# A state-space, attention and tree-router tower on one core: the last table doubling in two halves, and chunk 11 beside the first qkv step

## The chip, the core and the metric

The kernel runs on one core of a Trainium2 chip. Five engines work side by side: TensorE (PE) multiplies matrices, VectorE (DVE) and ScalarE (ACT) work on rows of 128 partitions, GpSimd (POOL) does elementwise work too, and SyncE (SP) mainly issues transfers. Each engine takes its instructions strictly in the order in which they were written for it, and waits for the others through semaphores. The metric is the device time of one execution in microseconds.

## The reference, cut to what matters

H = 256 channels, N = 64 states, 256 lags, 16 signals per channel. The output is a sum of three stages; the change touches the first and the place where it meets the second.

```
dA = (1 + dtA/2) / (1 - dtA/2)                 # one complex number z per channel and state
V  = exp(log(dA) * arange(256))                # its powers z^0 .. z^255
K  = 2 * real(einsum('chn,hnl->chl', C * B, V))     # the tokens: h
h  = h + attention_block(layernorm(h))         # norm, qkv, linear attention, proj, MLP
h  = h + tree_router(layernorm(h))
```

## The kernel before

**Tables.** A lag l is split into three digits, l = 64 d + 8 a + e with d < 4 and a, e < 8, so that z^l is a product of three table entries. `U` holds z^64, z^128 and z^192, `Er` and `Ei` hold z^1 to z^7, and `X` and `Y` (together `XY`, 8 values of each for every channel) hold B times z^(8a). The powers z, z^2, z^4 ... come from a chain of squarings between VectorE (L1088, L1090) and ScalarE (L662, L665). `X` and `Y` start with one value per channel and are doubled three times on VectorE (L1099 to L1120): 1 to 2, 2 to 4, 4 to 8 values, each time multiplied with a power that ScalarE has copied into PSUM. The last doubling is five instructions over all 256 channels. GpSimd makes z^3 (six instructions in `rotated`), then z^5 to z^7 for the first 128 channels (`shifted(0)`), then rotates chunks 0 and 1, then makes z^5 to z^7 for the other channels (`shifted(1)`).

**Fixed products.** Before the first chunk TensorE makes three products of weights alone: the gate's (L1715), the leaf values' (L1721) and a bias of the MLP (L1727, 16 groups of one column). It starts them when the weights' loads have landed and VectorE has passed a count (`DVE_POWERS + 8`). The first chunk's matmuls wait until ScalarE has copied the bias out of bank 0 (`b1copied`).

**Chunks.** The channels go in 16 chunks of 16. For each chunk n: SyncE loads the coefficients (`craw`, a direct and two crossed parts); GpSimd multiplies them with `U` into `Wa` and `Wb` (`rotate`, L514); ScalarE copies the chunk's `XY` to PSUM (`tables`), and the unrotated parts of `Wa` and `M` (`operands`); VectorE makes two products (L1130) and adds them into `M` (L1148, L1170); TensorE does 64 small matmuls (`tokens`, L1628); ScalarE copies the result to `tokev` (`token_row`, or `closed` with the store to a scratch in device memory). Chunk 10 is an exception: VectorE leaves its two products unadded (`unsummed_products`) and TensorE adds them with 128 matmuls instead of 64 (`unsummed_tokens`, L1646 and L1648).

**Steps.** The scratch is read back with the channels on the partitions (`load_h0`, tiles s = 0 to 15, of which 0 to 7 need chunks 0 to 7 only). A step s of the attention stage is: `norm1_stats(s)` on VectorE, `scales(s)` on GpSimd (three instructions, the last a power), `norm1_apply(s)` into `xh`, `y_transposes(s)` on TensorE, `y_high(s)` on ScalarE, `y_low(s)` on VectorE, then `q_products(s)` and `kv_products(s, 0 and 1)` on TensorE, with what ScalarE (`q_parts`, `kv_parts`) and VectorE (`q_elu`, `k_elu`) make of them. The chunks 12 to 15 run between steps 0 to 3. After them come the other steps, and then the loop of the MLP and the router.

**Order.** It is written by hand for each engine; nothing is moved by a scheduler. `CREDIT` is only a constant that is added to the loop semaphores. The names in what follows: W(n) is `rotate` of chunk n, M(n) the sum on VectorE, tokens(n) the matmuls.

## Time and profile before

| | us |
|---|---|
| time, median of 3 runs | 491.57 (491.56 to 491.72) |
| the profiled execution's own time | 492.88 |
| its span, first to last instruction | 491.1 |
| TensorE busy | 442.3 (90%) |
| VectorE busy | 346.6 (71%) |
| ScalarE busy | 294.8 (60%) |
| GpSimd busy | 191.5 (39%) |
| mean granted clock of TensorE | 0.968 of full |

The times below are microseconds from the start of the span. A row of the timeline gives start, duration, engine, line, operation, tiles and count, and in square brackets how long the engine had been idle before and what ended that. Operations on one engine overlap a little, so the step from one start to the next is a better price than the duration. Tile numbers are left out, so all banks of PSUM read as PS.

### The profile page before, as it was taken

How to read it: one execution, taken by the hardware profiler on the slowest of the kernel's cores; microseconds unless marked ns; L12 is line 12 of the kernel's file. 1: busy time of each engine (PE TensorE's matmuls, PEld its weight loads, DVE VectorE, ACT ScalarE, POOL GpSimd, SP SyncE). 2: the span in 40 equal slices, each digit the busy share in tenths (PEclk: the TensorE clock that was granted, in tenths of full speed). 3: DMA queues.
4: the chain of work that ended last, by engine and by line, in shares of the span. 5: the costliest groups of instructions: out<-in, count | busy, mean ns of one | idle time of the engine just before them, and what ended most of it. 6: DMA issues, size and time to landing. Idle time of an engine off the chain costs nothing.

```text
span 491.1 us, 11436 instructions
## 1 busy us (share of the span) xinstructions
PE 442.3 (90%) x3881; PEld 404.0 (82%) x3881; DVE 346.6 (71%) x814; ACT 294.8 (60%) x617; POOL 191.5 (39%) x188
## 2 busy tenths in 40 slices
PE   0475778999999999999999999999999999998995
PEld 0165667887888898988998998998998998998994
DVE  4899996996877785546586486486486576574675
ACT  4734654889876776466366366366367367356551
POOL 0299997742432110515405405406406306306120
PEclk9965999999999999999999999999999999999995
DMA  4532668445352111001002002002002001001002
GB/s 129 185 137 71 177 175 223 109 111 157 101 119 89 63 44 35 31 1 44 1 2 85 0 0 85 0 0 85 0 0 85 0 0 43 0 0 45 1 1 85
DMA packets 39903, 30.95 MB, mean 63 GB/s; under 512 B 19520, under 2 KB 35264, under 8 KB 39872
## 3 DMA queue, kind: packets, MB, share of 16 engines
q1 hardware_dynamic: 28944, 27.48, 18.9%
q10 hardware_dynamic: 10928, 3.08, 2.7%
q8 instruction: 16, 0.26, 0.2%
q14 instruction: 15, 0.12, 0.1%
...
## 4 chain that ended last, share of the span: by engine, by line
PE 69%; DVE 12%; issue 6%; POOL 4%; ACT 4%; DMA 3%; SPq 1%; DVEq 0%; POOLq 0%; ACTq 0%
PE PS L336 19%; PE PS L338 18%; PE PS L337 18%; PE PS L1655 5%; PE PS L1697 3%; PE PS L1628 2%; POOL Wb L514 2%; DVE XY L1055 2%; DVE bst L1357 2%; DMA craw<-in_c_ri 1%; DMA aim<-in_a_im 1%; PE PS L1664 1%; PE PS L1780 1%; DVE gl L1380 1%; DVE PS L1055 1%
## 5 line engine op out<-in xcount | busy, mean ns | idle before, releaser
L867 ACT ACTIVATE PS<-PS,fc1bias 128x512 f32<-128x512 f32 x56 | 36.7, 655 | 76.3 <-PE PS L338 76.2
L336 PE MATMUL PS<-fc2h,gh 128*128 128x256 f32 x256 | 74.7, 292 | 3.7 <-DVE gl L1380 2.3
L567 POOL TENSOR_SCALAR pst<-mv 128x4 f32<-128x4 f32 x15 | 4.2, 282 | 179.4 <-DVE pst L1364 179.4
L338 PE MATMUL PS<-fc2l,gh 128*128 128x256 f32 x256 | 71.4, 279 | 0.0
L337 PE MATMUL PS<-fc2h,gl 128*128 128x256 f32 x256 | 71.3, 278 | 0.0
L1380 DVE TENSOR_TENSOR gl<-PS,gh 128x512 fp32r<-128x512 f32 x56 | 38.6, 690 | 37.8 <-ACT gh L870 35.1
L336 PEld LDWEIGHTS PS<-fc2h,gh 128*128 128x128 f32 x256 | 48.0, 188 | 9.0 <-DVE gl L1380 3.0
L336 PE MATMUL PS<-x2Th,fc1h 128*128 (+2 forms) x144 | 54.5, 378 | 0.0
L337 PE MATMUL PS<-x2Th,fc1l 128*128 (+2 forms) x144 | 53.0, 368 | 0.0
L338 PE MATMUL PS<-x2Tl,fc1h 128*128 (+2 forms) x144 | 52.9, 367 | 0.0
L337 PEld LDWEIGHTS PS<-fc2h,gl 128*128 128x128 f32 x256 | 48.2, 188 | 0.8
L338 PEld LDWEIGHTS PS<-fc2l,gh 128*128 128x128 f32 x256 | 48.1, 188 | 0.0
L1628 PE MATMUL PS<-M,Wa 128*64 128x64 f32 x480 | 32.0, 233 | 11.7 <-ACT Wa L717 4.3
L1628 PEld LDWEIGHTS PS<-M,Wa 128*64 128x64 f32 x480 | 29.8, 143 | 14.4 <-issue 9.6
L870 ACT ACTIVATE gh<-PS 128x512 fp32r<-128x512 f32 x56 | 33.5, 599 | 2.8
L1628 PE MATMUL PS<-M,Wb 128*64 128x64 f32 x480 | 31.5, 230 | 0.0
L338 PEld LDWEIGHTS PS<-x2Tl,fc1h 128*128 128x128 f32 x144 | 27.1, 189 | 4.7
L1628 PEld LDWEIGHTS PS<-M,Wb 128*64 128x64 f32 x480 | 29.8, 146 | 0.0
L336 PEld LDWEIGHTS PS<-x2Th,fc1h 128*128 128x128 f32 x144 | 27.2, 189 | 2.5
L337 PEld LDWEIGHTS PS<-x2Th,fc1l 128*128 128x128 f32 x144 | 27.2, 189 | 2.3
L514 POOL TENSOR_TENSOR Wa<-craw,U 128x768 f32<-128x768 f32 x16 | 26.0, 1623 | 3.4 <-DMA craw<-in_c_ri 1.5
L336 PE MATMUL PS<-qkvh,yh 128*128 128x512 f32 x64 | 26.4, 412 | 0.0
(256 smaller groups left out, 1412.9 us busy)
## 6 DMA issues: line engine op xcount, KB each, us to landing
...
```

What stands on the lines that cost most here:

```text
L336: pe.matmul(dst, ah, bh, start=start, stop=False, **kw)
L337: pe.matmul(dst, al, bh, start=False, stop=False, **kw)
L338: return pe.matmul(dst, ah, bl, start=False, stop=stop, **kw)
L514: pool.tensor_tensor(w[:, par, :, :, 1:ND].rearrange("p h c d -> p d h c"), c, u, ALU.mult).then_inc(wdone, 1)
L867: act.activation(bank(j % 2), bank(j % 2), ACT.Gelu, bias=fc1bias[:, j:j + 1]).then_inc(gact, 1)
L870: act.activation(gh[:, j % 2, :], bank(j % 2), ACT.Copy).then_inc(gact, 1)
L1055: link(dve.tensor_tensor(out_, a, b, op))
L1357: dve.bn_stats(bst[:, t, :], x[:, t, :]).then_inc(done, 1)
L1380: dve.tensor_tensor(gl[:, j % 2, :], bank(j % 2), gh[:, j % 2, :].bitcast(F32), ALU.subtract).then_inc(gldone, 1)
L1628: mm = pe.matmul(dst, w[:, par, i, :, :].rearrange("p c d -> p (c d)"), M[:, par, i, :, :].rearrange("p a e -> p (a e)"), start=x == 0, st ...
L1655: mm = pe.transpose(PS[:, b + k, t * P:(t + 1) * P], src[:, t, k * P:(k + 1) * P], ident)
L1697: mm = pe.matmul(PS[:, sums_bank(c), k * (P + 1):(k + 1) * (P + 1)], key, value, start=half == 0 and k == 0, stop=half == 1, skip_group_ch ...
```

## The change

It has six parts.

1. **First loads.** `aim` was loaded by two DMAs on ScalarE's queue. Now its two halves go on the two queues, in front of the 768 KB of `qkvraw`, and two of the four `btab` loads move to ScalarE's queue.
2. **Powers.** z^3 is made in `pw` and already after `DVE_Z + 6`, beside the chain of squarings; `shifted` reads `pw` and `pw4` and no longer waits for ScalarE's copies. Those eight copies to `Er` and `Ei` come later. Five imaginary parts are written to PSUM by VectorE, and ScalarE copies fewer of them.
3. **Last doubling in halves.** Channels 0 to 127 are doubled before chunk 0, channels 128 to 255 between M(7) and the products of chunk 8. ScalarE's `tables` of chunks 8 and 9 wait for that (`DVE_XY`).
4. **Chunk 10 is summed on VectorE** as the others are, and `unsummed_tokens` is gone.
5. **Chunk 11** goes behind step 0's first `kv_products` on TensorE. W(11) stands behind `scales(0)`, and `norm1_stats`, `norm1_apply`, `y_high` and `tables` are in another order.
6. **Waits and loads.** The fixed products start at `DVE_POWERS + 10`, and the last quarter of the bias's products waits for the first product of chunk 0. SyncE loads tile 0 of h0 before the coefficients of chunks 10 and 11, and the coefficients of chunk 12 before tiles 2 and 3.

```diff
-DVE_W1 = DVE_U + 3
+DVE_XY = DVE_U + 5
+DVE_W1 = DVE_XY + 3
 DVE_W2 = DVE_W1 + 2 + KD
 POOL_TABLES = 1 + 2 * 6
+GATE = 10
...
+        def u_imag(d):
+            return (PS[:, 2, H:2 * H], PS[:, 3, 0:H], PS[:, 3, H:2 * H])[d]
+
         def power(j):
 
-            if j < 3:
+            if j < 2:
                 return [pw[:, j, x, :] for x in range(2)]
+            if j == 2:
+                return [pw4[:, x, :] for x in range(2)]
             if j < 6:
-                return [pwb[:, j - 3, x, :] for x in range(2)]
-            return [U[:, 0, j - 6, :], ui[:, j - 6, :]]
+                return [pwb[:, j - 3, 0, :], (PS[:, 6, H:2 * H], PS[:, 7, H:2 * H], PS[:, 2, 0:H])[j - 3]]
+            return [U[:, 0, j - 6, :], u_imag(j - 6)]
...
-            sp.dma_start(qkvraw[:, :, :], qkvT.rearrange("(k p) o -> p k o", p=P)).then_inc(ld_qkv, 16)
+            sp.dma_start(aim[halves[1], :], a_im).then_inc(ld_aim, 16)
             for r, rows in enumerate(halves):
                 sp.dma_start(btab[rows, 0, :], b_ri[r]).then_inc(ld_b, 16)
-                sp.dma_start(btab[rows, 1, :], b_ri[1 - r]).then_inc(ld_b, 16)
+            sp.dma_start(qkvraw[:, :, :], qkvT.rearrange("(k p) o -> p k o", p=P)).then_inc(ld_qkv, 16)
...
-            for n in range(2, FIRST):
+            for n in range(2, SINGLE):
                 load_c(n // 2, n % 2)
             for par in range(2):
                 sp.wait_ge(h0st[par], CREDIT + 16 * (PAIRS // 2))
-            for s in range(4):
+            load_h0(0)
+            for n in range(SINGLE, FIRST):
+                load_c(n // 2, n % 2)
+            load_h0(1)
+            load_c(FIRST // 2, FIRST % 2)
+            for s in range(2, 4):
                 load_h0(s)
-            load_c(FIRST // 2, FIRST % 2)
             store_h0(SINGLE)
...
-            pool.wait_ge(dve_set, DVE_POWERS)
-            rotated(Er[:, :, 2], Ei[:, :, 2], pw[:, 0, 0, :], pw[:, 0, 1, :], pw[:, 1, 0, :], pw[:, 1, 1, :],
+            pool.wait_ge(dve_set, DVE_Z + 6)
+            rotated(pw[:, 2, 0, :], pw[:, 2, 1, :], pw[:, 0, 0, :], pw[:, 0, 1, :], pw[:, 1, 0, :], pw[:, 1, 1, :],
                     tE[:, :, 0])
-            pool.wait_ge(e_out, 6)
-            wr, wi = (pw[:, 2, x, :].unsqueeze(2).to_broadcast([P, H, 3]) for x in range(2))
+            wr, wi = (pw4[:, x, :].unsqueeze(2).to_broadcast([P, H, 3]) for x in range(2))
 
             def shifted(half):
                 hs = slice(half * P, (half + 1) * P)
-                rotated(Er[:, hs, 4:7], Ei[:, hs, 4:7], Er[:, hs, 0:3], Ei[:, hs, 0:3], wr[:, hs, :], wi[:, hs, :],
-                        tE[:, hs, :])
+                ar, ai = (pw[:, :, x, hs].rearrange("p e h -> p h e") for x in range(2))
+                rotated(Er[:, hs, 4:7], Ei[:, hs, 4:7], ar, ai, wr[:, hs, :], wi[:, hs, :], tE[:, hs, :])
...
             rotate(SINGLE // 2, 0)
-            rotate(SINGLE // 2, 1)
             scales(0)
             pool.wait_ge(xh1, CREDIT + 2)
+            rotate(SINGLE // 2, 1)
             rotate(FIRST // 2, 0)
...
             act.dma_start(iar[N:P, :], inv_ar).then_inc(ld_exp, 16)
+            act.dma_start(aim[0:N, :], a_im).then_inc(ld_aim, 16)
             for r in range(2):
-                act.dma_start(aim[r * N:(r + 1) * N, :], a_im).then_inc(ld_aim, 16)
+                act.dma_start(btab[r * N:(r + 1) * N, 1, :], b_ri[1 - r]).then_inc(ld_b, 16)
...
+            act.activation(PS[:, 6, 0:H], pwb[:, 0, 0, :], ACT.Copy).then_inc(pw_out, 1)
+            act.wait_ge(dve_set, DVE_POWERS + 4)
             for d in range(ND - 1):
-                if d == 2:
-                    act.wait_ge(dve_set, DVE_POWERS + 4)
-                act.activation(U[:, 1, d, :], ui[:, d, :], ACT.Copy, scale=sgn[:, 0:1]).then_inc(u_out, 1)
-
+                act.activation(U[:, 1, d, :], u_imag(d), ACT.Copy, scale=sgn[:, 0:1]).then_inc(u_out, 1)
+            act.activation(pwb[:, 2, 1, :], PS[:, 2, 0:H], ACT.Copy).then_inc(u_out, 1)
+            act.activation(PS[:, 7, 0:H], pwb[:, 1, 0, :], ACT.Copy).then_inc(pw_out, 1)
...
+            act.wait_ge(pool_set, 1 + 6)
+            for e in range(4):
+                for x, t in enumerate((Er, Ei)):
+                    w = pw4[:, x, :] if e == 3 else pw[:, e, x, :]
+                    act.activation(t[:, :, e], w, ACT.Copy).then_inc(e_out, 1)
...
+            act.activation(PS[:, 6, H:2 * H].rearrange("p (x h) -> p x h", x=2), pwb[:, 2, :, P:H],
+                           ACT.Copy).then_inc(pw_out, 1)
+            act.wait_ge(pe_set, 2)
+            act.activation(leafraw[:, :, :].rearrange("p k x -> p (k x)"), bank(5), ACT.Copy).then_inc(staged, 1)
...
+            with act.Fori(0, 2) as it:
                 for par in range(2):
                     next_opened(it, par)
-            paired_tables(4, 1)
+            next_opened(2, 0)
+            paired_operands(3, 1)
+            closed(2, 1)
+            m_unshifted(3, 1)
             closed(3, 0)
             paired_operands(4, 0)
+            closed(3, 1)
+            act.wait_ge(dve_set, DVE_XY)
+            for par in range(2):
+                paired_tables(4, par)
             m_unshifted(4, 0)
-            closed(3, 1)
             paired_operands(4, 1)
             m_unshifted(4, 1)
             tables(SINGLE)
+            closed(SINGLE // 2 - 1, 0)
             operands(SINGLE)
-            closed(SINGLE // 2 - 1, 0)
-            tables(SINGLE + 1)
             closed(SINGLE // 2 - 1, 1)
             operands(SINGLE + 1)
+            tables(SINGLE + 1)
+            y_high(0)
+            tables(SINGLE + 2)
             token_row(SINGLE)
-            tables(SINGLE + 2)
             operands(SINGLE + 2)
-            y_high(0)
             for n in range(FIRST, CHUNKS):
                 s = n - FIRST
+                if s == 0:
+                    q_parts(s)
...
+            dve.wait_ge(pw_out, 1)
+            doubled(slice(0, H), 1, *halves_of(6), bank(0))
+            dve.wait_ge(pw_out, 2)
+            dve.wait_ge(u_out, 4)
+            doubled(slice(0, H), 2, *halves_of(7), PS[:, 2:4, :].rearrange("p b x -> p (b x)"))
+            dve.wait_ge(pw_out, 3)
+            doubled(slice(0, P), 4, *(w[:, 0:P] for w in halves_of(1)), bank(2))
...
-            for n in range(6, SINGLE - 1):
-                overlapped(n, n % 2)
-            product_sums(SINGLE - 1, 1)
+            overlapped(6, 0)
+            product_sums(7, 1)
+            dve.wait_ge(pw_out, 4)
+            doubled(slice(P, H), 4, PS[:, 6, H:H + P], PS[:, 6, H + P:2 * H], bank(2))
+            assert count[0] == DVE_XY, count[0]
+            dve.wait_ge(pool_set, POOL_TABLES + 6)
+            for n in (8, 9):
+                first_product(n, n % 2)
+                second_product(n, n % 2)
+                product_sums(n, n % 2)
...
-            unsummed_products(SINGLE)
+            norm1_stats(0)
+            single_product(SINGLE, 0)
+            single_product(SINGLE, 1)
+            single_sums(SINGLE)
+            norm1_apply(0)
             single_product(SINGLE + 1, 0)
             single_product(SINGLE + 1, 1)
-            norm1_stats(0)
+            y_low(0)
             single_sums(SINGLE + 1)
-            norm1_apply(0)
             norm1_stats(1)
-            norm1_stats(2)
-            y_low(0)
             for n in range(FIRST, CHUNKS):
                 s = n - FIRST
                 single_product(n, 0)
+                if s == 0:
+                    norm1_stats(2)
+                    norm1_apply(1)
                 single_product(n, 1)
+                single_sums(n)
                 if s == 0:
-                    norm1_apply(1)
                     norm1_apply(2)
...
-            pe.wait_ge(dve_set, DVE_POWERS + 8)
+            pe.wait_ge(dve_set, DVE_POWERS + GATE)
...
+                if j == JH * 3 // 4:
+                    pe.wait_ge(prodX, CREDIT + 1)
...
-            unsummed_tokens(SINGLE)
             y_transposes(0)
-            pe.wait_ge(tokout, CREDIT + SINGLE + 1)
-            tokens(SINGLE + 1, 1, None)
+            pe.wait_ge(tokout, CREDIT + SINGLE - 1)
+            tokens(SINGLE, 0, 0)
             pe.wait_ge(qkvld, 3)
             for n in range(FIRST, CHUNKS):
                 s = n - FIRST
                 if s > 0:
                     y_transposes(s + 1)
                 q_products(s)
+                if s == 0:
+                    pe.wait_ge(tokout, CREDIT + SINGLE)
                 kv_products(s, 0)
                 if s == 0:
+                    pe.wait_ge(tokout, CREDIT + SINGLE + 1)
+                    tokens(SINGLE + 1, 1, 0)
                     y_transposes(s + 1)
                 kv_products(s, 1)
                 pe.wait_ge(tokout, CREDIT + n)
-                tokens(n, n % 2, None)
+                tokens(n, n % 2, 0)
```

VectorE, from M(7) on, in the kernel before (XY is the table, PS the banks, Mb and Mc hold second products, bst and mv the statistics of a tile of h0):

```order
L1130 TENSOR_TENSOR Mb<-PS,Ei 128x896 [waits vdone]
L1130 TENSOR_TENSOR PS<-PS,Er 128x896 [waits vdone,xyld]
L1148 TENSOR_TENSOR M<-PS,Mb 128x128x7 [waits prodY,prodX,tokmm]
L1130 TENSOR_TENSOR Mc<-PS,Ei 128x896 [waits vdone]
L1148 TENSOR_TENSOR M<-PS,Mc 128x128x7 [waits prodY,prodX,tokmm]
L1130 TENSOR_TENSOR M<-PS,Er 128x128x7 [waits vdone,tokmm,xyld]
L1130 TENSOR_TENSOR Mc<-PS,Ei 128x896
```

And now, from M(7) to M(8):

```order
L1177 TENSOR_TENSOR M<-PS,Mc 128x128x7 [waits prodY,prodX,tokmm]
L1074 TENSOR_TENSOR XY<-XY,PS 128x256x4 [waits pw_out]
L1074 TENSOR_TENSOR PS<-XY,PS 128x512 [waits dve_set]
L1074 TENSOR_TENSOR XY<-XY,PS 128x128x4 [waits dve_set]
L1074 TENSOR_TENSOR PS<-XY,PS 128x512 [waits dve_set]
L1074 TENSOR_TENSOR XY<-XY,PS 128x128x4 [waits dve_set]
L1159 TENSOR_TENSOR PS<-PS,Er 128x896 [waits xyld,vdone,pool_set,dve_set]
L1159 TENSOR_TENSOR Mb<-PS,Ei 128x896 [waits vdone]
L1177 TENSOR_TENSOR M<-PS,Mb 128x128x7 [waits prodY,prodX,tokmm]
```

Five instructions of the doubling stand between M(7) and chunk 8, and chunk 8's products are no longer made ahead of the sum before them.

GpSimd from W(11) on, in the kernel before (Wa and Wb make one W; pst and mr are `scales`):

```order
L514 TENSOR_TENSOR Wa<-craw,U 128x3x256 [waits tokmm,cld1]
L514 TENSOR_TENSOR Wb<-craw,U 128x3x256 [waits crossld1]
L522 ISA
L522 TENSOR_SCALAR pst_94<-mv_93 128x2 [waits st1]
L523 TENSOR_SCALAR pst_94<-mv_93 128x2
L525 TENSOR_TENSOR mr<-pst_94,halfpow 128x2x2 [waits r1done]
L514 TENSOR_TENSOR Wa<-craw,U 128x3x256 [waits cld0,xh1,tokmm]
```

And now, from behind W(10) on:

```order
L529 ISA
L529 TENSOR_SCALAR pst_94<-mv_93 128x2 [waits st1]
L530 TENSOR_SCALAR pst_94<-mv_93 128x2
L532 TENSOR_TENSOR mr<-pst_94,halfpow 128x2x2 [waits r1done]
L521 TENSOR_TENSOR Wa<-craw,U 128x3x256 [waits cld1,xh1,tokmm]
L521 TENSOR_TENSOR Wb<-craw,U 128x3x256 [waits crossld1]
L521 TENSOR_TENSOR Wa<-craw,U 128x3x256 [waits tokmm,cld0]
L521 TENSOR_TENSOR Wb<-craw,U 128x3x256 [waits crossld0]
L529 TENSOR_SCALAR pst_94<-mv_93 128x2 [waits st1]
```

`scales(0)` has moved in front of W(11), which now stands together with W(12) behind the wait for step 0's `xh`.

## Rows read from the trace of the kernel before

**Rows 1.** Busy time of each engine in a stretch, then TensorE's granted clock.

```profile
97.00:103.80 6.80, 6.80 (x94) 5.98 (x92) 6.63 (x15) 5.96 (x15) 4.61 (x6) 1.00 0.45 122
```

**Rows 2.** Chain that ended last: start, us, what.

```profile
1.97 6.12 DMA aim<-in_a_im
...
88.12 2.10 PE PS L1628 x64
90.23 0.59 PE PS L1664 x4
```

**Rows 3.** Timeline of VectorE, from the tables to step 0.

```profile
6.04 0.43 DVE L1068 SCALAR_TENSOR_TENSOR base<-base 128x256 f32<-128x256 f32 x1 [3.41 <-ACT base L644]
8.18 0.42 DVE L1070 SCALAR_TENSOR_TENSOR base<-aim,base 128x256 f32<-128x256 f32 x1 [1.72 <-DMA aim<-in_a_im]
...
27.53 0.69 DVE L1055 TENSOR_TENSOR XY<-XY,PS 128x512 f32<-128x512 f32 x1
...
28.97 3.54 DVE L1055 TENSOR_TENSOR XY<-XY,PS 128x1024 f32<-128x1024 f32 x2
32.55 1.23 DVE L1055 TENSOR_TENSOR PS<-XY,PS 128x1024 f32<-128x1024 f32 x1
...
38.17 1.10 DVE L1130 TENSOR_TENSOR PS<-PS,Er 128x896 f32<-128x896 f32 x1 [0.62 <-ACT PS L722]
39.18 1.08 DVE L1130 TENSOR_TENSOR Mb<-PS,Ei 128x896 f32<-128x896 f32 x1
...
78.26 0.74 DVE L1213 TENSOR_SCALAR xh<-h,mv,mr 128x256 f32<-128x256 f32 x2 [0.83 <-issue]
...
84.52 0.74 DVE L1213 TENSOR_SCALAR xh<-h,mv,mr 128x256 f32<-128x256 f32 x2
...
86.89 1.08 DVE L1170 TENSOR_TENSOR M<-PS,Mb 128x896 f32<-128x896 f32 x1
```

**Rows 4.** Timeline of TensorE: gate product, tokens(0), tokens(8).

```profile
27.03 3.78 PE L1715 MATMUL PS<-routraw,wqraw 128*128 128x256 f32 x8 [9.35 <-DMA fc1raw<-in_fc1T]
...
41.63 0.49 PE L1628 MATMUL PS<-M,Wa 128*64 128x64 f32 x4 [3.93 <-DVE M L1148]
...
66.95 0.34 PE L1628 MATMUL PS<-M,Wa 128*64 128x64 f32 x4 [0.89 <-POOL Wb L514]
```

**Rows 5.** TensorE in stretches: length, busy, granted clock, DMA.

```profile
17.70:22.00 4.30, 0.00 (x0) 1.00 0.82 232
23.00:27.00 4.00, 0.00 (x0) 0.50 1.01 377
27.00:33.00 6.00, 5.97 (x14) 0.50 0.38 131
...
42.00:45.00 3.00, 3.00 (x62) 0.50 0.16 52
64.00:66.00 2.00, 2.00 (x64) 1.00 0.69 183
```

**Rows 6.** Timeline of GpSimd: W(2), W(10), `scales(0)`, W(12), `scales(1)`, W(13).

```profile
45.72 1.61 POOL L514 TENSOR_TENSOR Wa<-craw,U 128x768 f32<-128x768 f32 x1 [0.64 <-PE PS L1628]
...
69.53 1.63 POOL L514 TENSOR_TENSOR Wa<-craw,U 128x768 f32<-128x768 f32 x1
...
76.54 0.24 POOL L522 TENSOR_SCALAR pst<-mv 128x2 f32<-128x2 f32 x1 [0.96 <-DVE mv L1205]
...
79.64 1.64 POOL L514 TENSOR_TENSOR Wa<-craw,U 128x768 f32<-128x768 f32 x1 [1.48 <-DMA craw<-in_c_ri]
...
82.82 0.22 POOL L522 TENSOR_SCALAR pst<-mv 128x2 f32<-128x2 f32 x1
...
87.18 1.62 POOL L514 TENSOR_TENSOR Wa<-craw,U 128x768 f32<-128x768 f32 x1 [1.04 <-DVE xh L1213]
```

**Rows 7.** Timeline of ScalarE: token row of chunk 7, what follows its store.

```profile
66.16 0.60 ACT L736 ACTIVATE tokev<-PS 128x512 f32<-128x512 f32 x1 [0.88 <-PE PS L1628]
...
67.30 0.71 ACT L717 ACTIVATE Wa<-craw 128x256 f32<-128x256 f32 x1 [0.55 <-ACT tokev L736]
```

87 lines of the change are left out of this document (27 added, 60 removed).

## The prediction

> **What bounds the kernel now.** I first read the busy time by stretches. From 97.0 to 103.8 us TensorE is busy 6.80 of 6.80 us at full clock [rows 1], and the chain that ended last has TensorE in it from tokens(12) at 88.12 and `y_transposes(2)` at 90.23 on [rows 2]. From there the order of work is the same in both kernels. So the change is worth what `y_transposes(2)` comes earlier, and the question is what holds the time before it. The timelines answer that. Up to 38 us it is VectorE's tables, behind `aim`, which lands 6.12 us after its issue [rows 2, 3]. Then GpSimd sets the pace: W(2) starts at 45.72, when tokens(0) is done, and W(10) at 69.53, eight chunks in 23.81 us, 2.98 each, without a wait [rows 6]. VectorE has three operations for each chunk, 1.0 us apart [rows 3], so it has no slack to speak of. After W(11) it is a load, `scales` and `xh`: W(12) waits for its coefficients until 79.64, `scales(1)` starts at 82.82, `xh(1)` at 84.52, M(12) at 86.89 [rows 3, 6].
>
> **The first loads.** VectorE is ready for `aim` at 6.04 + 0.43 = 6.5 and starts at 8.18 [rows 3]. The gain is between 0 and 1.67 us. The half that landed late was issued third on its queue, while 768 KB ran on the other. Both halves are now ahead of that block, and their nearest neighbour is `iar`, issued just ahead, which had landed and been used by 6.04 [rows 3]. I take 1.67.
>
> **The half doubling.** The last doubling is now 2.31 us (3.54 less the 1.23 of the step before) and four of 1.23, together 7.2. Half of it is one of 1.23 and four of 0.69 [rows 3], with gaps 4.1. So the first product comes 3.2 us earlier, at 38.17 - 1.67 - 3.2 = 33.3, and VectorE would let tokens(0) start at 41.63 - 4.85 = 36.8 [rows 3, 4]. z^3 and the first shift on GpSimd hide behind this, since they start nine VectorE steps of 0.43 sooner and the 1.67 besides: 5.5 us. ScalarE's late copies of `Er` and `Ei` hide in the time in which it has nothing else before the first `tables`. I cost both at nothing; without the cover each would hold up the first product.
>
> **The fixed products take over as the bound of tokens(0).** Before they started at 27.03, when `fc1raw` had landed, and ended 3.93 us ahead of tokens(0), at 37.7 [rows 4]. Now they wait for the load and for the second instruction of the second doubling: 27.53 + 0.69 - 1.67 = 26.55. They start at 26.7 at the earliest and end at 37.4; with the copy of the bias tokens(0) would start at 37.8. But from 27 to 33 us the clock was at 1.2 GHz [rows 5]. That is six us of their 10.7, so a rise two us sooner saves one. The bounds are 36.8 (VectorE) and 37.8. I take 37.0, near the lower, because the rise in this trace came only 6 us after their start, and leaves more room for an earlier one than for a later.
>
> **tokens(0) to W(10).** At half clock tokens(0) starts 4.09 us before W(2) [rows 4, 6]; at full clock 64 matmuls take 2.1 [rows 2], so this would be 2.7. In the trace tokens(0) ran at 0.50 [rows 5], 3.93 us behind the bias products, which stream one column each; the pause is gone now, the thin products ahead of it are not. I take half again: W(2) at 41.1, 4.6 earlier. GpSimd is free by then: its own work ended at 45.72 - 0.64 = 45.1, and by the 5.5 us above now ends at 39.6. The same 4.6 us hold up to chunk 7: its token row moves from 66.16 to 61.55 [rows 7]. Here the second half costs. ScalarE's next operation comes 1.14 us after the start of the token row, behind the store [rows 7]: `tables(8)` at 62.7. VectorE has done M(7) at 57.5 (24 operations since 33.3, and 0.2) and the doubling at 61.6, so the 4.1 us are hidden behind TensorE and ScalarE. But chunk 8's products, which were made ahead before, start only now: 0.6 us behind `tables` (0.62 at 38.17), and from the first product to the matmuls it is 3.3 more (41.63 - 38.17, less a short wait) [rows 3, 4]. tokens(8) starts at 66.6 against 66.95. Of 4.6 us there are 0.35 left.
>
> **The new gap on TensorE.** Between tokens(7), done at 61.4, and tokens(8) TensorE now stands still for 5.2 us; before it was 0.89 [rows 4]. In the stretches the clock was full from 17.7 to 22 us, in a pause that began at 17.7, and at half from 23 on: after some 5.3 us [rows 5]. The pauses of 0.9 us between chunks left it full, as from 64 to 66. So I take the clock to fall in the gap, and tokens(8) to run at half: W(10) comes 4.1 us behind its start, at 70.7, against 69.53. At full clock it would be at 69.3. The Trainium skill, "TensorE: Matmul & The Clock Gate", section on HAM oscillation, says that bursts of matmuls with waits between them let the clock fall back, so that each burst begins slow. That speaks against this change at this place. By the page's rule the sum is the one taken here; if the clock took no note of the gap, as it took none of the pauses of 0.89 us, it would be 1.4 us less.
>
> **W(10) to the steady steps.** The chain of prices: from W to the `scales` behind it 3.18 (79.64 to 82.82); `scales` to `xh` 1.72 (76.54 to 78.26); `xh` to the next W 0.94 [rows 3, 6]; a W 2.98. So `scales(0)` is at 73.9, `xh(0)` 75.6, W(11) 76.55, W(12) 79.5, `scales(1)` 82.7, `xh(1)` 84.4. The load for W(12) is now issued before two tiles of h0 and no longer waited for. Behind `xh(1)` stand 0.7 us of its own and the second product, 1 us, which has moved there: M(12) at 86.2 against 86.89. Then `xh(2)`, 0.6 us, has moved between M(12) and `y_low(1)`, so `y_transposes(2)` waits for that and starts at 89.6 against 90.23 [rows 2]. Chunk 10's sum on VectorE is another 1 us, and spares TensorE the 64 extra matmuls; both lie under the wait for `xh(0)`, which GpSimd's `scales(0)` sets. Chunk 11's 2 us between the two `kv_products` fit in, because TensorE would wait for `xh(1)` there.
>
> **Sum.** 90.23 - 89.6 is 0.6 us, of a profiled execution of 492.88. The timed runs have a median of 491.57, 1.3 lower; I apply the difference to the median: **490.9 us** (0.65 earlier, the rounding of the steps). A difference under 0.2%, 1.0 us, is about what a measurement of this kernel can't tell from no change.
>
> **Rivals.**
>
> A. *The clock stays up.* If tokens(8) runs at full clock, W(10) and all that follows come 1.4 us earlier: 489.5. If tokens(0) does too, up to another 1.4: 488.1. For it: the clock did not fall in the short pauses. Against it: the falls in rows 5 and the length of the gap.
>
> B. *The clock falls a second time, slower in the end.* Between tokens(9) and `xh(0)` TensorE has a second pause of 3 us. If tokens(10) runs at half clock, with the transposes ahead of it 0.6 us longer, it ends at 76.4 + 1.2 + 3.7 = 81.3. W(12) needs it done, and 0.64 us more: 81.9 in place of 79.5. That is 2.4 us: 493.3. It decides from the point where tokens(10) ends after 78.9. The pause is shorter than the one that lowered the clock, which speaks against it.
>
> C. *`aim` lands no earlier.* Then the first product is at 35.0 and the fixed products start at 28.3 and end near 38.7: tokens(0) at 39, 2.0 later than forecast, and all the rest with it: 492.9. For it: the same bytes are loaded in the first 8 us whatever the order. Against it: the late half was the one behind the large block.
>
> **How the numbers follow.** Forecast 0.42, its own range 490.0 to 491.9, from tokens(0) at 36.8 or 37.8 and 0.5 us for the new order of ScalarE. Rival A 0.25, B 0.20, C 0.13. The range is 488.8 to 493.2; it leaves out half of A's second part and the end of B. Faster by over 0.2% means below 490.6: all of A and 0.17 of the forecast, 0.42. Slower means above 492.55: most of B and of C, 0.23. Between them 0.35.
>
> **What would show it.** In the profile of the changed kernel: the second instruction on `aim` at 6.5; the first product near 33.3; tokens(0) at 37.0 at clock 0.50 and W(2) at 41.1; five instructions on XY between 57.5 and 61.6, `tables(8)` at 62.7; tokens(8) at 66.6 with 5 us of pause before it and the clock at half in it; W(10) at 70.7; no wait of W(12) for a load; M(12) at 86.2; `y_transposes(2)` at 89.6, then steps of 6.8 us as before. The prediction is wrong if the clock in tokens(8) is full, if W(10) waits for the tile of h0 that is now loaded before its coefficients, or if VectorE's second half is not done when ScalarE comes to `tables(8)`.

## The result, and the profile after

The changed kernel takes **493.3 us** (median of 20 runs, 491.38 to 496.71), the kernel before, run beside it on the same chip, 491.89 us (20 runs, 490.31 to 492.83). The ratio is 1.0036, with a 95% interval of 1.0023 to 1.0049: slower by 0.36%, 1.8 us by the ratio. The forecast was 490.9, the range ended at 493.2. It is the time of rival B, but B's reason turned out to be only part of it.

The 20 runs spread over 5.3 us, twice the spread before, and they go with TensorE's mean granted clock. The three at 0.976 took 491.38 to 491.81 us, the six at 0.972 491.81 to 492.69, the nine from 0.969 to 0.964 492.79 to 495.08, the two at 0.960 and 0.958 496.61 and 496.71. The profiled execution is in the better half: 492.69 us, span 490.7, clock 0.972.

VectorE's timeline of the changed kernel (start, duration, engine, line, operation, tiles, idle time before) beside [rows 3]:

```profile
6.37 0.42 DVE L1089 SCALAR_TENSOR_TENSOR base<-aim,base 128x256 f32<-128x256 f32 x1
...
33.17 1.10 DVE L1159 TENSOR_TENSOR PS<-PS,Er 128x896 f32<-128x896 f32 x1 [0.65 <-ACT PS L729]
...
57.58 1.21 DVE L1074 TENSOR_TENSOR XY<-XY,PS 128x1024 f32<-128x1024 f32 x1
...
61.01 0.69 DVE L1074 TENSOR_TENSOR XY<-XY,PS 128x512 f32<-128x512 f32 x1
62.80 1.10 DVE L1159 TENSOR_TENSOR PS<-PS,Er 128x896 f32<-128x896 f32 x1 [1.11 <-ACT PS L729]
```

The tables went as worked out: no wait for `aim` at 6.37, the first product at 33.17 (forecast 33.3), the second half of the doubling done at 61.7 (61.6), chunk 8's first product at 62.80. TensorE's timeline beside [rows 4]:

```profile
27.33 3.78 PE L1727 MATMUL PS<-routraw,wqraw 128*128 128x256 f32 x8 [11.44 <-DMA fc1raw<-in_fc1T]
...
37.13 0.34 PE L1659 MATMUL PS<-M,Wa 128*64 128x64 f32 x4 [0.78 <-ACT b1add L810]
...
66.26 0.49 PE L1659 MATMUL PS<-M,Wa 128*64 128x64 f32 x4 [5.25 <-DVE M L1177]
75.92 1.08 PE L1676 MATMUL PS<-const,xh 128*128 128x128 f32 x4 [3.07 <-issue]
```

tokens(0) is at 37.13 (37.0). It begins at full clock (0.34 us for its first four products, where [rows 4] have 0.49 at half), so W(2) comes 3.47 us behind it and not the 4.1 of the forecast. Then come the two pauses, 5.25 us ahead of tokens(8) and 3.07 ahead of `y_transposes(0)`. These four transposes take 1.08 us; at full clock four of them take 0.66, in the row at 85.80 further down. TensorE by stretches (length, busy, instructions, granted clock, DMA), where 1.00 is 2.4 GHz and 0.50 is 1.2:

```profile
62.00:65.00 3.00, 0.00 (x0) 1.00 0.44 87
65.00:68.00 3.00, 1.74 (x33) 0.54 0.62 185
68.00:71.00 3.00, 3.00 (x62) 0.50 0.59 165
71.00:74.00 3.00, 1.86 (x45) 0.82 0.58 131
74.00:77.00 3.00, 1.08 (x6) 0.75 0.81 195
77.00:80.00 3.00, 3.00 (x66) 0.69 0.40 119
80.00:83.00 3.00, 3.00 (x21) 1.00 0.47 96
```

In the kernel before all of these stretches are at 1.00. Here the clock falls in the first pause, comes back at about 72, falls again at about 76 and is back only in tokens(10), at about 79. So both falls are in this run. GpSimd beside [rows 6]:

```profile
40.60 1.63 POOL L521 TENSOR_TENSOR Wa<-craw,U 128x768 f32<-128x768 f32 x1 [1.06 <-PE PS L1659]
...
70.18 1.61 POOL L521 TENSOR_TENSOR Wa<-craw,U 128x768 f32<-128x768 f32 x1 [5.70 <-PE PS L1659]
...
80.15 1.61 POOL L521 TENSOR_TENSOR Wa<-craw,U 128x768 f32<-128x768 f32 x1 [1.05 <-PE PS L1659]
```

W(10) at 70.18 (forecast 70.7), but W(12) at 80.15 (79.5): it waits for tokens(10), as rival B says. And then, where the prediction took both kernels to be the same, another row is different. VectorE, GpSimd and TensorE behind `xh(1)`, and last tokens(14) in the kernel before:

```profile
85.00 0.73 DVE L1242 TENSOR_SCALAR xh<-h,mv,mr 128x256 f32<-128x256 f32 x2 [1.68 <-issue]
85.66 1.08 DVE L1159 TENSOR_TENSOR Mb<-PS,Ei 128x896 f32<-128x896 f32 x1
86.87 1.09 DVE L1191 TENSOR_TENSOR M<-PS,Mb 128x896 f32<-128x896 f32 x1
```

```profile
88.81 1.66 POOL L521 TENSOR_TENSOR Wa<-craw,U 128x768 f32<-128x768 f32 x1 [2.19 <-DVE xh L1242]
```

```profile
85.80 0.66 PE L1676 MATMUL PS<-const,xh 128*128 128x128 f32 x4 [0.78 <-DVE xh L1242]
...
90.28 0.63 PE L1676 MATMUL PS<-const,xh 128*128 128x128 f32 x4
...
102.51 0.34 PE L1659 MATMUL PS<-M,Wa 128*64 128x64 f32 x4 [0.42 <-DVE M L1191]
```

```profile
101.75 0.34 PE L1628 MATMUL PS<-M,Wa 128*64 128x64 f32 x4
```

M(12) is level with before (86.87 against 86.89), `y_transposes(2)` too, 0.1 us later (90.28 against 90.16 in the same view of before). But at 102.51 tokens(14) waits for M(14), and it is 0.8 us later than before, where no such wait is (101.75). From `y_transposes(2)` to tokens(14) it is 12.23 us here and 11.59 before. On the way `xh(2)` is 1.6 us later than before (87.88 against 86.24), and so is W(13), which waits for it (88.81 against 87.18 [rows 6]). At 475 us the kernel is still 0.8 us behind (the transposes of the last half's `x` at 475.21 against 474.41). Its span is nevertheless 0.4 us shorter, since the last stretch was at full clock here (first fence) and at half before (second):

```profile
485.00:489.00 4.00, 2.01 (x15) 0.99 0.57 197
```

```profile
485.00:489.00 4.00, 2.90 (x12) 0.50 0.43 148
```

So the one profiled execution alone would have misled: it is faster than that of before by 0.2 us, with a good start (W(2) at 40.60, second best of seven profiled executions with this start) and a good tail by chance, while the medians differ by 1.4 us the other way.

### The profile page after: what moved, and what is told of

Same layout as the page of the kernel before. It is cut to its first block, busy times and chain, and to the rows that moved or that the text cites. A ratio compares the mean times of both kernels' runs of the same rounds, so it can differ in the third digit from the quotient of the medians.

```text
span 490.7 us, 11307 instructions
## 1 busy us (share of the span) xinstructions
PE 439.3 (90%) x3817; PEld 401.4 (82%) x3817; DVE 348.9 (71%) x820; ACT 296.5 (60%) x621; POOL 192.2 (39%) x188
## 4 chain that ended last, share of the span: by engine, by line
PE 70%; DVE 12%; issue 6%; ACT 4%; POOL 3%; DMA 2%; DVEq 0%; SPq 0%; POOLq 0%; ACTq 0%
PE PS L340 19%; PE PS L342 18%; PE PS L341 18%; PE PS L1667 5%; PE PS L1659 3%; PE PS L1709 3%; DVE bst L1389 2%; DMA fc1raw<-in_fc1T 2%; POOL Wb L521 1%; PE PS L1676 1%; PE PS L1797 1%; DVE gl L1412 1%; DVE PS L1159 1%; DVE Mb L1159 1%; DMA iar<-in_inv_ar 1%
## 5 line engine op out<-in xcount | busy, mean ns | idle before, releaser
L1659 PE MATMUL PS<-M,Wa 128*64 128x64 f32 x512 | 36.5, 243 | 12.4 <-DVE M L1177 5.6
L1659 PEld LDWEIGHTS PS<-M,Wa 128*64 128x64 f32 x512 | 34.0, 152 | 15.6 <-issue 10.7
L1659 PE MATMUL PS<-M,Wb 128*64 128x64 f32 x512 | 35.9, 239 | 0.0
L1659 PEld LDWEIGHTS PS<-M,Wb 128*64 128x64 f32 x512 | 34.0, 155 | 0.0
```

The costliest lines, as they stand in the source:

```text
L1659: mm = pe.matmul(dst, w[:, par, i, :, :].rearrange("p c d -> p (c d)"), M[:, par, i, :, :].rearrange("p a e -> p (a e)"), start=x == 0, st ...
```

## Experiments

Each was timed in five rounds beside the kernel before, whose median was 491.4 to 492.1 in all of them. They ran on several chips; where runs of different groups are compared, the ratios to the kernel before are the safer measure. *Fillings* are products of 128x512 whose results nobody reads (the operands are float32r; the first expectation calls them bf16):

```diff
+            def fill(count, b=0):
+                for _ in range(count):
+                    pe.matmul(bank(b), qkvh[:, 0, 0:P], qkvh[:, 0, 0:512], start=True, stop=True)
```

### The two pauses: fill both, the first, the second

```diff
-            with pe.Fori(0, SINGLE // 2) as it:
+            with pe.Fori(0, SINGLE // 2 - 1) as it:
...
+            pe.wait_ge(tokout, CREDIT + SINGLE - 3)
+            fill(21)
+            for n in range(SINGLE - 2, SINGLE):
+                pe.wait_ge(tokout, CREDIT + n - 1)
+                tokens(n, n % 2, n % 2)
             pe.wait_ge(staged, 1)
+            pe.wait_ge(tokout, CREDIT + SINGLE - 1)
+            fill(12)
             y_transposes(0)
-            pe.wait_ge(tokout, CREDIT + SINGLE - 1)
```

> The changed kernel with work for TensorE in its two new pauses: 21 products of 128x512 (bf16, into the bank that tokens(8) overwrites) ahead of tokens(8), 12 ahead of y_transposes(0). Their results are not used; nothing is left out. Theory (the clock): the loss against the forecast, and the spread from 491.4 to 496.7 us, come from a TensorE clock that falls in these pauses, at a moment that differs from run to run. Then tokens(8) runs at full clock, W(10) comes at 69.0 in place of 70.18, W(12) at 78 in place of 80.15, the median is 489.5 to 490.5 us and the runs spread no more than those of the kernel before (2.5 us). Rival (the order of chunks 10 and 11 on VectorE and GpSimd costs the time): the clock is full and the median stays within 1 us of 493.3. Rival (the fillings themselves hold tokens(8) up): W(10) later than 70.2 and slower than the changed kernel.

> The changed kernel with the 21 products ahead of tokens(8) alone. Theory (the clock, both pauses): tokens(8) runs at full clock, and the pause ahead of y_transposes(0) grows from 3 to more than 4 us and can still lower it, so W(12) waits for tokens(10) in some runs: a median of 490.5 to 492 and a spread of 3 us or more. If the first pause is all that matters: 489.5 to 490.5 with a small spread, as with both filled. If only the second matters: 493.3 still.

> The changed kernel with the 12 products ahead of y_transposes(0) alone, the pause ahead of tokens(8) left empty. Theory (each pause costs by itself): filling the first gave 1.4 us, filling both 2.35, so filling the second alone gives about 1: 492.3, with tokens(8) still at half clock in most runs and tokens(10) at full. Rival (the second fall follows from the first, so that with the clock already low the fillings only add work): 493.3 or more. Rival (the second pause is all): 491.0, as with both filled.

Measured: both 490.95 us (12 runs, 489.82 to 492.42; ratio 0.9985, interval 0.9972 to 0.9997), the first alone 491.89 (ratio 1.0010, 0.9993 to 1.0026), the second alone 492.31 (1.0022, 1.0005 to 1.0039). From 493.3 that is 2.35, 1.4 and 1.0 us; by the ratios 2.5, 1.3 and 0.7. The interval of the second alone overlaps that of the changed kernel, so the second pause is shown by another pair, timed side by side: with the first filled, filling the second too takes 491.89 to 490.95 (the means lie 1.2 apart). So each pause costs by itself, and the medians add up. With both filled the runs spread 2.6 us, as before.

The rows agree. From W(2) to W(10) it is 29.6 us in the changed kernel and with the second pause filled, 27.9 with both filled and 28.0 with the first. From W(10) to W(12), where 8.8 was forecast, it is 9.97 in the changed kernel, 11.51 with the first filled, 8.85 with the second, 9.60 with both (0.65 of it a wait for a load). The first expectation asked for more than came: W(10) is at 70.26, not 69.0, behind a W(2) at 42.34, and the median is 0.45 above its range.

 TensorE with both filled, then with the first alone, where TensorE stands still for 3.54 us ahead of `y_transposes(0)`:

```profile
65.00:68.00 3.00, 2.73 (x14) 1.00 0.52 104
...
77.00:80.00 3.00, 2.50 (x69) 1.00 0.57 168
```

```profile
68.00:71.00 3.00, 1.89 (x64) 1.00 0.66 181
71.00:74.00 3.00, 1.02 (x35) 1.00 0.68 165
74.00:77.00 3.00, 1.44 (x12) 0.57 0.88 218
77.00:80.00 3.00, 3.00 (x62) 0.50 0.24 73
```

Extra work on the engine that was thought to be the bottleneck makes the kernel faster, with the order of everything else unchanged: what is won back is the clock's. The Trainium skill, "TensorE: Matmul & The Clock Gate", section on HAM oscillation, says that waits between bursts of matmuls let the clock fall back; the trace agrees (0.54 from 65 to 68 us with the first pause empty, 1.00 with it filled). But the 489.5 of rival A was not reached: 1.5 us stayed open. One part showed in GpSimd's rows, with both pauses filled:

```profile
70.26 1.62 POOL L521 TENSOR_TENSOR Wa<-craw,U 128x768 f32<-128x768 f32 x1 [4.07 <-PE PS L1663]
72.53 1.60 POOL L521 TENSOR_TENSOR Wb<-craw,U 128x768 f32<-128x768 f32 x1 [0.65 <-DMA craw<-in_c_ri]
```

### The queue of loads

The coefficients of chunk 10 now stand behind SyncE's wait for the store of chunk 7. In this run they go out first, with both pauses filled:

```diff
-            for n in range(2, SINGLE):
+            for n in range(2, FIRST):
                 load_c(n // 2, n % 2)
             for par in range(2):
                 sp.wait_ge(h0st[par], CREDIT + 16 * (PAIRS // 2))
             load_h0(0)
-            for n in range(SINGLE, FIRST):
-                load_c(n // 2, n % 2)
```

> The changed kernel with both pauses filled as before (21 and 12 products whose results are not used), and SyncE issuing the coefficients of chunks 10 and 11 ahead of its wait for the stores of chunks 6 and 7 again, as the kernel before does. Theory (with the clock up, the second multiplication of W(10) waits 0.65 to 0.70 us for its coefficients, since they were queued behind that wait): that wait is gone, and all behind it comes 0.6 to 0.8 us earlier: 490.2 against 490.95 with the filling alone. Rival (the first tile of h0 now lands too late for the statistics of step 0): no gain.

Measured: 491.11 us (ratio 0.9996, 0.9980 to 1.0012). The wait of 0.65 us is gone, and from W(10) to W(11) it is 5.87 us against 6.64. The median shows nothing of it; the two intervals overlap, and 0.7 us is too little to tell.

### The doubling whole again

```diff
-            doubled(slice(0, P), 4, *(w[:, 0:P] for w in halves_of(1)), bank(2))
+            doubled(slice(0, H), 4, *halves_of(1), PS[:, 2:4, :].rearrange("p b x -> p (b x)"))
...
-            doubled(slice(P, H), 4, PS[:, 6, H:H + P], PS[:, 6, H + P:2 * H], bank(2))
```

> The changed kernel with the last doubling whole ahead of chunk 0 again, and the products of chunks 8 and 9 made ahead as in the kernel before; the loads, the table stage and the new order of chunks 10 and 11 stay. Theory (the clock in the pause that the second half makes): no pause ahead of tokens(8); first product at 36.4, tokens(0) at 40.3, W(10) at 67.5 to 68.2, no fall of the clock there, a median of 490 to 491 and a spread near 2.5 us. Rival (the order of chunks 10 and 11 costs): 492 or more although W(10) is early.

> The last doubling whole ahead of chunk 0, the other parts of the change kept, and the coefficients of chunks 10 and 11 loaded ahead of SyncE's wait for the stores. Theory (the 4.1 us for which W(10) waited in the run with the old load order is the price of that queue): W(10) starts at 67.6 to 68.5 without a wait, xh(0) 4 us earlier, and the median falls by 3.5 to 4 us from 494.2 to 490.3. Rival (the new order of chunks 10 and 11 is what costs): 492 or more.

> The same with 14 products (128x512, results unused) ahead of y_transposes(0). Theory (that pause of about 3.5 us lowers the clock in some runs): tokens(10) always at full clock, median 0.5 to 1 us below the same kernel without them, near 489.6, and a smaller spread. Rival (the whole doubling has no pause long enough): the same median within 0.4 us.

Measured: 494.23 us (ratio 1.0052, 1.0033 to 1.0070), 495.04 (1.0078, 1.0060 to 1.0097) and 495.87 (1.0097, 1.0077 to 1.0117). All three expectations fell, and the third's rival with it (within 0.4 us; it is 0.8 slower). GpSimd in the first, VectorE in the second:

```profile
71.87 1.57 POOL L521 TENSOR_TENSOR Wa<-craw,U 128x768 f32<-128x768 f32 x1 [4.13 <-DMA craw<-in_c_ri]
```

```profile
73.62 0.76 DVE L1214 BATCH_NORM_STATS2 bst<-h 128x6 f32<-128x256 f32 x2 [7.08 <-DMA h<-h_scratch]
```

Without the pause GpSimd reaches W(10) at 67.7, but then the queue bites. With tile 0 of h0 first, the coefficients are 4.1 us late. With the coefficients of both chunks first, the tile is late, and since the change `xh(0)` stands ahead of W(11), so `xh(0)` comes at 77.78 against 75.08. So without the pause the wait moves to the loads, and the kernel is slower than with it; what the pause costs can't be read from these runs. The second has the number of its rival (the new order costs), which the run with the old order answers below. The third run filled a pause that lasts 8 us: the products ran from 70.27 for 3.5 us, TensorE then stood still for 4.55, and the transposes behind it took 1.12 us, at half clock.

### The first loads alone, on the kernel before

```diff
+            sp.dma_start(aim[halves[1], :], a_im).then_inc(ld_aim, 16)
...
-            for r in range(2):
-                act.dma_start(aim[r * N:(r + 1) * N, :], a_im).then_inc(ld_aim, 16)
+            act.dma_start(aim[0:N, :], a_im).then_inc(ld_aim, 16)
```

> The kernel before with the new order of the first loads alone. By the prediction's step: the second instruction on aim starts 1.7 to 1.8 us earlier, the first product at 36.5, tokens(0) at 40, W(2) at 44.0 and all behind it 1.7 us earlier: 490.2 against 491.9 of the kernel before. Rival (the fixed products then bound tokens(0), or a fall of the clock comes at another place): less than 0.8 us of gain.

Measured: 490.81 us (ratio 0.9984, 0.9969 to 0.9999), 1.17 below its own before; by the ratio 0.8, with an interval that ends just below 1. `aim` is not waited for (6.41), but the first product comes at 37.00, 1.17 earlier and not 1.67. The rest is at the squarings:

```profile
12.78 0.42 DVE L1056 TENSOR_TENSOR pw<-PS,base 128x256 f32<-128x256 f32 x1 [1.01 <-ACT base L659]
```

Half a microsecond goes to a wait of 1.01 us for ScalarE, which is copying `qkvh`. In the kernel before and in the changed kernel this wait is 0.40.

### The old order of chunks 10 and 11

```diff
             rotate(SINGLE // 2, 0)
+            rotate(SINGLE // 2, 1)
             scales(0)
             pool.wait_ge(xh1, CREDIT + 2)
-            rotate(SINGLE // 2, 1)
...
-            y_transposes(0)
             pe.wait_ge(tokout, CREDIT + SINGLE - 1)
             tokens(SINGLE, 0, 0)
+            y_transposes(0)
```

> The changed kernel with the old order of chunks 10 and 11 on three engines: GpSimd multiplies W(11) ahead of scales(0), TensorE runs tokens(10) ahead of y_transposes(0), ScalarE takes the token row of chunk 10 ahead of y_high(0). VectorE still adds chunk 10. Theory (the second pause with its fall of the clock costs 1 us, and the order as such is neutral: xh(0) comes 3 us later, but only one W is left behind it): W(10) at 70.2, W(11) at 73.2, scales(0) at 76.2, xh(0) at 77.9, W(12) at 78.9 against 80.15; tokens(10) splits the pause; 492 to 493. Rival (the new order, with xh(0) at 75.1, is what the change gains by): W(12) later than 80.2 and 494 or more, as where the whole doubling came first.

Measured: 496.8 us (ratio 1.0083, 1.0060 to 1.0105), 3.5 us slower than the changed kernel, 2.3 by the ratios. The forecast of "neutral" is wrong. `xh(0)` falls back to 80.07, 7.85 us behind W(10) instead of 4.90, and with it `y_low(0)` and the statistics of step 1 on VectorE, for which `scales(1)` then waits 2.42 us (86.46 against 83.30; 2.0 of these 3.2 us are the later W(10) of this execution, 72.22). Not all of the loss is the order by itself: TensorE stands still for 3.10 us ahead of `y_transposes(0)` and 2.56 behind them, and its clock is at 0.50 from 83 to 86 us, where the changed kernel has 1.00. The new order as such does not make the changed kernel slow.

### The start and the tail

Fillings at the start. The first two runs are the changed kernel with both pauses filled and the early loads: one with 6 ahead of the fixed products and 9 behind the bias products, one with 8 ahead and one before each of the first six pairs of bias products. The third is the kernel before with the new first loads, 5 ahead, one before each of the eight pairs and 8 behind. In the last two VectorE's first product of chunk 1 also waits for the fillings, which use its bank. Each has 7 fillings of 128x256 ahead of the last product of the kernel. The fourth has those 7 alone, on the kernel before. The edit of the first:

```diff
+            pe.wait_ge(qkvld, 1)
+            fill(6, 4)
             pe.wait_ge(ld_w1, 16 * 5)
...
             pe.wait_ge(b1copied, 1)
+            fill(9)
...
             last_lT(0)
+            for _ in range(7):
+                pe.matmul(last_bank(0), fc2h[:, 0, 0:P], fc1h[:, 0, 0:HT], start=True, stop=True)
             last_leaf(0)
```

> The changed kernel with the coefficients of chunks 10 and 11 loaded early, both pauses filled, and three more fillings: 6 products ahead of the fixed products (once bank 4 is free), 9 between the bias products and tokens(0), 7 ahead of the last product of the kernel. Results unused, nothing left out. Theory (the clock is also down behind the pauses at 17 to 27 us and near the end, at a moment that differs from run to run): tokens(0) at 36.8 to 37.2 at full clock, W(2) at 39.6 in place of 40.6 to 42.3, all behind it as much earlier, 0.5 us in the tail: 488.5 to 489.2. Rival (the start is bound by VectorE and the load, whatever the clock): the same as with two fillings and the early loads.

> The changed kernel with early loads of the coefficients of chunks 10 and 11 and both pauses filled, and besides: 8 products ahead of the fixed products (their start overlaps the wait for the load), one 128x512 product ahead of each of the first six pairs of bias products, and 7 ahead of the last product of the kernel. Results unused, nothing left out. Theory (what is left against rival A of the prediction, some 1.5 us, is the clock from 22 to 44 us: the fixed products start at half clock, and it falls again under the one-column bias products, so tokens(0) runs at half): tokens(0) at 36.8 to 37.3 at full clock, W(2) at 39.6 to 40.2 in place of 42.7, median 488.5 to 489.2. Rival (the extra products lengthen the fixed products so far that tokens(0) is later than 38.2): 491 or more.

> The kernel before with the new order of the first loads, and wide products whose results are not used: 5 ahead of the fixed products, one ahead of each pair of bias products, 8 behind them, 7 ahead of the last product of the kernel. Theory (in the kernel before tokens(0) too runs at half clock, and VectorE, not TensorE, holds it): tokens(0) at the same 40.5 but at full clock, W(2) at 43.1 in place of 44.5, the tail 0.5 us shorter: 488.9 to 489.5 against 490.8 with the loads alone. Rival (the clock at the start does not matter since something else holds W(2)): 490.8 less 0.5.

> The kernel before with 7 products (128x256, results unused) ahead of its last product. Theory (part of the spread of both kernels, 2.5 us in the kernel before, is a clock that falls or not in the pauses of the last 10 us): the median falls by 0.5 to 1.2 us, to 490.8 or less, and the slowest runs go. Rival (the spread comes from the start alone): the same as the kernel before within 0.3 us.

Measured: 491.18 us (ratio 0.9996, 0.9981 to 1.0011), 489.74 (0.9960, 0.9943 to 0.9976), 492.12 (1.0021, 1.0008 to 1.0035) and, the tail alone, 490.96 (0.9973, 0.9960 to 0.9986). The tail is settled: with 7 small products the kernel before gains 0.7 us by the medians and 1.3 by the ratio, and nine runs lie between 489.96 and 491.21, where the 20 beside them lie between 490.4 and 493.06. In its profiled execution the clock is at 1.00 from 480 to 489 us, in that of the kernel before at 0.54 and then 0.50. The start is a lesson in overshooting. TensorE in the first of these runs:

```profile
37.53 4.21 PE L1649 MATMUL PS<-qkvh 128*128 128x512 f32 x9 [0.27 <-ACT b1add L808]
41.67 0.49 PE L1661 MATMUL PS<-M,Wa 128*64 128x64 f32 x4
```

There is no pause to fill between the bias products and tokens(0). Nine fillings at half clock take 4.2 us, and tokens(0) starts at 41.67. The third run made the same mistake (tokens(0) behind eight at half clock, 3.76 us, at 42.77), and so lost what it could have gained. The second had only the six fillings between the bias products. Its clock stayed at 1.00 from 33 to 39 us, but tokens(0) came at 39.13, as its rival says; its gain over 491.11 is 1.4 us, of which the tail's fillings explain 0.7 to 1.3. All three missed their expected times. The tail alone fell by an amount in its range of 0.5 to 1.2 us.

### The bias products moved, then split

First all eight pairs of bias products went into the pause ahead of tokens(8), behind seven fillings, with six more ahead of tokens(0). Then five stayed ahead of tokens(0), each behind one filling, and three went into the pause behind ten, with the coefficients of chunk 10 ahead of SyncE's wait and those of chunk 11 behind tile 0 of h0. Both with the second pause and the tail filled. The edit of the second:

```diff
+            def bias(j):
+                fill(1, 1)
                 for k in range(KD):
...
+            pe.wait_ge(dve_set, DVE_U)
+            for j in range(5):
+                mm = bias(j)
...
+            fill(10)
+            pe.wait_ge(tokout, CREDIT + SINGLE - 2)
+            for j in range(5, JH):
+                mm = bias(j)
```

> The changed kernel with the bias products (fc1raw times nrm) moved out of the way of tokens(0) into the pause between tokens(7) and tokens(8), with 7 wide products ahead of them; 6 wide products ahead of tokens(0), 12 ahead of y_transposes(0), 7 ahead of the last product of the kernel; coefficients of chunks 10 and 11 loaded early. Nothing left out. Theory (with the pauses filled the rest of the loss is the start: fixed products that end late because the clock rises late, and tokens(0) at half clock behind one-column products): tokens(0) follows VectorE, at 36.6 to 37.2 in every run, W(2) at 39.6 to 40.5, W(10) 2.5 to 3 us earlier than in the run with both pauses filled (70.3), and the median is 487.5 to 488.5. Rival (W(2) and what follows are held by something else): 489.7 as with the earlier fillings, or more.

> The changed kernel with the bias products split: five of the eight pairs ahead of tokens(0), each behind one wide product, and three in the pause ahead of tokens(8) behind 10 wide ones; 14 wide products ahead of y_transposes(0), 7 ahead of the last product of the kernel; the coefficients of chunk 10 loaded ahead of SyncE's wait for the stores, the first tile of h0 behind that wait and ahead of chunk 11's. Nothing left out. Theory (the start, the two pauses and the tail are clock; in the run that moved all bias products the start was right, with tokens(0) at 36.3 and W(2) at 39.9, and the loss came from thin products in the first pause and from the late tile of h0): tokens(0) at 36.6 to 37.3, W(10) at 68.5 to 69.5 without a wait for a load, VectorE's first statistics not waiting for h0, xh(0) near 73.5, median 488 to 489. Rival (filling with wide products costs as much as it gives here, or W(10) is held by something else): 489.7 or more.

Measured: 493.05 us (ratio 1.0027, 1.0010 to 1.0043) and **488.91** (0.9937, 0.9917 to 0.9956). In the first the start is right, tokens(0) at 36.34 and W(2) at 39.92, but in the pause the one-column products take 4.53 us, the clock falls in that time, and tokens(8) starts at 67.31 at half clock; the expected 487.5 to 488.5 us are missed by far. The bias products of the first, then the second run by stretches, then its GpSimd:

```profile
61.96 4.53 PE L1749 MATMUL PS<-nrm,fc1raw 128*128 128x1 f32 x32
```

```profile
36.00:39.00 3.00, 2.22 (x58) 1.00 0.41 114
...
65.00:68.00 3.00, 2.96 (x68) 1.00 0.46 136
```

```profile
68.27 1.61 POOL L520 TENSOR_TENSOR Wa<-craw,U 128x768 f32<-128x768 f32 x1 [4.05 <-PE PS L1664]
```

In the second run tokens(0) is at 37.45 (expected 36.6 to 37.3), W(10) at 68.27 with no wait for a load (68.5 to 69.5), `xh(0)` at 73.18 (73.5), the time in its range. It changes the start, the pauses, two loads and the tail together; what each gives of its 3.1 us is not separated.

### The second product of chunk 12

```diff
                     norm1_stats(2)
-                    norm1_apply(1)
                 single_product(n, 1)
+                if s == 0:
+                    norm1_apply(1)
                 single_sums(n)
```

> The changed kernel with chunk 12's second product ahead of norm1_apply(1) on VectorE again, as in the kernel before. Theory (the last 0.7 us: VectorE, not TensorE, carries the chain from xh(1) at 85.00 to tokens(14) at 102.51, because the product of 1.0 us that was made in the wait for scales(1) now stands behind xh(1)): the product goes into VectorE's 1.68 us of waiting, xh(1) stays where it is, tokens(14) does not wait for M(14), and the median falls by 0.5 to 0.8 us, to 492.5 to 492.8. Rival (TensorE has slack enough there, so the order on VectorE does not matter): 493.3 within the spread.

> The kernel with the bias products split and the pauses filled (488.91), with that same move. There VectorE waits only 0.80 us ahead of xh(1), so the product of 1.0 us puts xh(1) off by about 0.2. Theory: 0.3 to 0.6 us faster, 488.3 to 488.6. Rival (xh(1) is what counts): 0.2 slower.

Measured: 492.32 us on the changed kernel (ratio 1.0013, 0.9994 to 1.0032), 1.0 below it, and **488.05 us** on the split one (5 runs, 487.62 to 488.68; ratio 0.9922, 0.9903 to 0.9940), 0.9 below 488.91. Both gained a little more than expected, but in both pairs the intervals of the ratios overlap. The rows are sharper. From `y_transposes(2)` to tokens(14) it is 12.23 us in the changed kernel and in the split one, and 11.59 in both with this move, as in the kernel before: 0.64 us. TensorE in the first run:

```profile
90.49 0.66 PE L1677 MATMUL PS<-const,xh 128*128 128x128 f32 x4
...
102.08 0.34 PE L1660 MATMUL PS<-M,Wa 128*64 128x64 f32 x4
```

VectorE in the first, and the busy time by stretches in the changed kernel (first row) and with this move (second row: TensorE, its loads, VectorE, ScalarE, GpSimd, clock):

```profile
83.80 1.06 DVE L1159 TENSOR_TENSOR Mb<-PS,Ei 128x896 f32<-128x896 f32 x1
85.66 0.73 DVE L1242 TENSOR_SCALAR xh<-h,mv,mr 128x256 f32<-128x256 f32 x2 [0.80 <-issue]
86.31 1.09 DVE L1191 TENSOR_TENSOR M<-PS,Mb 128x896 f32<-128x896 f32 x1
```

```profile
97.00:104.00 7.00, 6.47 (x84) 5.53 (x82) 6.48 (x14) 5.97 (x15) 4.47 (x5) 1.00 0.44 116
```

```profile
97.00:104.00 7.00, 7.00 (x105) 6.17 (x101) 6.48 (x15) 5.93 (x15) 4.49 (x5) 1.00 0.44 117
```

The product fits into VectorE's wait for `scales(1)`, M(12) starts 0.65 us behind `xh(1)` instead of 1.87, and TensorE has no more idle time from 97 to 104 us.

## Why the prediction was wrong, point by point

- **First loads, -1.67.** Right for `aim`. Alone on the kernel before they bring the first product 1.17 us forward, since the squarings then wait for ScalarE; in the changed kernel the first product is where it was forecast.
- **The half doubling, first product at 33.3.** Right (33.17), as are the hiding of z^3, of the shift and of the late copies.
- **tokens(0) at 37.0, the step with too narrow bounds.** It is 37.13 in the profiled run. In the six other profiled executions with the same start it is 36.62 (the second product moved), 37.03 (the first pause filled), 37.95 (the second), 38.25 (both), 38.57 (the old order) and 38.60 (both and the early loads): four of seven are above the bound of 37.8, one is below 36.8. W(2) is at 40.16, 40.60, 40.97, 42.04, 42.34, 42.66 and 42.69; the mean, 41.6, is 0.5 us behind the 41.1 of the forecast. The fixed products were priced from one run in which the clock came back at 33, with the argument that there was more room for an earlier rise. What was not weighed is that it falls again: in the run with the second pause filled it was up from 32 to 35, where the one-column bias products run, and down again to 42.
- **tokens(8) at 66.6, the fall in the 5 us pause, W(10) at 70.7.** Right: 66.26, half clock, 70.18. Filling this pause gives the 1.4 us that the prediction names for it (1.3 by the ratios, 1.5 to 1.7 by the rows from W(2) to W(10)).
- **W(10) to W(12), the step that failed first.** The forecast left the clock up in the second pause of 3 us, because it was shorter than the one of 5, and so put the wait of W(12) for tokens(10) at nothing. In the profiled run the clock falls there (0.75 and 0.69 at 74 to 80 us), tokens(10) ends late, and W(12) comes at 80.15 in place of 79.5: 9.97 us behind W(10), forecast 8.8. Filling the pause is worth 1.0 us (0.7 to 1.2 by other measures), not rival B's 2.4. The full price does occur: with the first pause filled alone W(12) is 11.51 us behind W(10). But it is not paid in every run. The mechanism stood among the rivals with its place right; its chance of 0.20 and its price as a fixed amount were both off. That rival B's 493.3 is the measured median is therefore luck: 1.0 of its 2.4 us is its own, the rest comes from the start and from the second product. That a pause is shorter than one that lowered the clock was no reason to leave the clock up.
- **W(12) without a wait for its load.** Right, but what the same edit did to chunk 10 was left out. Its coefficients are now queued behind a wait for chunk 7's store; GpSimd waits 0.65 us for them as soon as the clock is up (the median shows nothing of it), and 4.1 us without the pause. The prediction named this as something that would make it wrong, and did not price it.
- **"From there the order of work is the same in both kernels."** Wrong, and the one step that no rival covered. The second product of chunk 12 was noted as moved and its 1 us counted up to M(12), but not beyond, and "steps of 6.8 us as before" is 7.49 from tokens(13) to tokens(14). VectorE is busy 6.63 of 6.80 us there in the kernel before [rows 1], TensorE 6.80, so little can be made up: the microsecond surfaces as the later `xh(2)` and W(13) and in the end as the wait of TensorE for M(14). Undoing this one move gives 0.64 us in the rows and 0.7 to 1.0 in the times. The path between M(12) and M(14) is read from the rows, and it holds a gap of 0.48 us on VectorE ahead of M(14) whose cause is not shown; tested is only what the move costs at its end.
- **M(12) at 86.2, y_transposes(2) at 89.6.** 86.87 and 90.28: both are late by 0.7 us, and 0.65 of it is W(12); the prices behind it held.
- **The sum.** 0.5 (start) + 1.0 (second pause) + 0.6 to 1.0 (second product) is 2.1 to 2.5 on top of the -0.65 of the forecast: +1.5 to +1.9 against the +1.4 by medians and the +1.8 by the ratio. The three come from few runs and are good to some 0.8 us each, so the agreement is no closer than that. That the median of before was taken as 491.57 from three runs, where 20 give 491.89, is another 0.3 of the 2.4 us between forecast and result.

Open is what decides, from run to run, when the clock falls and comes back. The runs show only that it is not the same moment each time, and that wide products in these two pauses kept it up. Two parts of the change were not tested alone: the new making of the powers, and chunk 10's sum on VectorE. For the second the row of `xh(0)` speaks: VectorE stands still for 1.61 us ahead of it, until GpSimd's `scales(0)` is done, so in that execution the sum is hidden.
